# The fifth product of an expert's first layer over 128 rows of the weight tail in place of 64

## The reference

```
# layer 0: 16 experts, hidden width 384, top 4 by softmax
h = einsum('nh,ech->nec', t, mlp1_w) + mlp1_b        # 192 -> 768 (gate and linear part)
a = min(glu, 7) * sigmoid(1.702 * glu) * (clip(lin, -7, 7) + 1)
out = sum_e comb[n, e] * (a_e @ mlp2_w_e.T + mlp2_b_e)   # 384 -> 192
# layer 1: 8 experts, hidden width 768, top 1
out = sum_e comb[n, e] * (relu(x @ wi_e) @ wo_e)         # 192 -> 768 -> 192
```

## Time and profile before

| | |
|---|---|
| median of 3 runs | 606.01 us (605.06 to 611.18) |
| the profiled execution: span, first to last instruction | 613.5 us (the page gives no other time of it) |
| matmuls busy | 536.5 us, 87% of the span |
| weight loads busy | 444.9 us, 73% |
| DVE busy | 349.5 us, 57% |
| ACT, POOL busy | 213.7 us, 170.6 us |
| up(0) of layer 0 starts, layer 0's last add ends | 123.9 us, 368.9 us |
| up(0) of layer 1 starts, last down ends | 446.9 us, 610.7 us |

### The profile page before, as it was taken

The page is one execution under the profiler, slowest core; times in us unless marked ns, Lnnn a source line. Parts: engine busy times, 40 slices in busy tenths (PEclk is TensorE's granted clock), DMA queues, the critical chain, the costliest instruction groups (busy, mean ns, idle before and its releaser), DMA issues.

```text
span 613.5 us, 9611 instructions
## 1 busy us (share of the span) xinstructions
PE 536.5 (87%) x3471; PEld 444.9 (73%) x3471; DVE 349.5 (57%) x678; ACT 213.7 (35%) x344; POOL 170.6 (28%) x104
## 2 busy tenths in 40 slices
PE   5799969699899999999999997602597999999998
PEld 5446956487788888888888883202385998899988
DVE  1340156558687877877777663997527733333332
ACT  0011131245355455455455431702223234223230
POOL 1100021205244444444444114240004442144110
PEclk9755558689799999999999986555558999999999
DMA  8200001002222222222222310010001202221001
GB/s 334 91 0 0 1 1 52 1 1 72 72 72 71 71 71 71 71 71 71 73 88 88 124 41 0 0 51 1 1 0 65 92 25 91 91 90 38 1 1 28
DMA packets 8843, 33.41 MB, mean 54 GB/s; under 512 B 961, under 2 KB 1762, under 8 KB 8818
## 3 DMA queue, kind: packets, MB, share of 16 engines
q1 hardware_dynamic: 8674, 33.00, 15.7%
q10 hardware_dynamic: 144, 0.07, 0.1%
HBM read 32.65 MB, written 0.42 MB: 54 GB/s over the span
## 4 chain that ended last, share of the span: by engine, by line
PE 63%; DVE 11%; issue 1%; ACT 1%; DVEq 0%
PE ps L1194 35%; PE ps L1056 26%; DVE hs L977 1%; DVE prod L972 1%; DVE rmat L957 1%; DVE aval L842 1%; DVE h L806 1%; DVE stats L580 1%; PE ps L1041 0%; PE ps L1045 0%; DVE rmat L961 0%; DVE above L658 0%; DVE bsq L948 0%; DVE qx L944 0%; PE ps L1248 0%
## 5 line engine op out<-in xcount | busy, mean ns | idle before, releaser
L525 POOL TENSOR_TENSOR w_lo<-raw,w_hi 128x768 fp32r<-128x768 f32 x48 | 100.1, 2108 | 310.1 <-ACT w_hi L329 310.1
L1056 PE MATMUL ps<-w_hi,hid_hi 128*119 128x192 f32 (+1 forms) x480 | 129.3, 269 | 0.0
L1056 PE MATMUL ps<-w_lo,hid_hi 128*119 128x192 f32 (+1 forms) x480 | 127.4, 265 | 0.0
L1056 PE MATMUL ps<-w_hi,hid_lo 128*119 128x192 f32 (+1 forms) x480 | 127.3, 265 | 0.0
L1056 PEld LDWEIGHTS ps<-w_hi,hid_hi 128*119 128x119 f32 (+1 forms) x480 | 84.7, 176 | 3.5 <-issue 0.4
L806 DVE SCALAR_TENSOR_TENSOR h<-ps,comb,h 119x192 f32<-119x192 f32 (+1 forms) x120 | 49.8, 415 | 65.1 <-PE ps L1056 61.7
L1056 PEld LDWEIGHTS ps<-w_lo,hid_hi 128*119 128x119 f32 (+1 forms) x480 | 84.7, 176 | 0.0
L1056 PEld LDWEIGHTS ps<-w_hi,hid_lo 128*119 128x119 f32 (+1 forms) x480 | 84.6, 176 | 0.0
L1194 PE MATMUL ps<-xa_hi,w_hi 128*128 128x272 f32 x288 | 76.6, 349 | 7.2 <-DVE hid_lo L1012 3.9
L1194 PE MATMUL ps<-xb_hl,w_lo 64*128 64x272 f32 x288 | 76.6, 347 | 0.0
L1012 DVE SCALAR_TENSOR_TENSOR hid_lo<-ps,hid_hi 128x544 fp32r<-128x544 f32 x48 | 34.6, 725 | 55.2 <-ACT hid_hi L499 55.1
(11 more groups left out here) (183 smaller groups left out, 704.0 us busy)
## 6 DMA issues: line engine op xcount, KB each, us to landing
raw<-in_w SPq DMA_DIRECT2D x24, 768.0 KB, 5.5
raw<-in_w SPq DMA_DIRECT2D x16, 288.0 KB, 2.8
raw<-in_w SPq DMA_DIRECT2D x8, 576.0 KB, 3.8
xp_sb<-in_xp SPq DMA_DIRECT2D x4, 357.0 KB, 5.6
pk_sb<-in_pk SPq DMA_DIRECT2D x1, 970.0 KB, 8.2
pk_sb<-in_pk SPq DMA_DIRECT2D x1, 851.5 KB, 9.0
tokw_sb<-in_tokw SPq DMA_DIRECT2D x1, 672.0 KB, 4.5
out_rows<-h SPq DMA_DIRECT2D x4, 89.2 KB
```

Of the source, the lines that this page charges most:

```text
L525: pool.tensor_tensor(w1_lo[k][:, a:a + W1C], raw1[k][:, a:a + W1C], w1_hi[k][:, a:a + W1C].bitcast(F32), ALU.subtract).then_inc(s["w1_lo"], 1)
L1056: ins = pe.matmul(dst, a, b, start=(n == 0), stop=(n == len(pairs) - 1), skip_group_check=True)
```

## The change

The last entry of `parts` takes all 128 rows of both operands: `w1_lo[:, b]` against `xb_hl[:]`. Rows 64 to 127 add lo(weight)·lo(token) of the tail to the sum, a product that was left out before. The count, the order, the columns and the waits of all matmuls stay as they are; 24 experts x 6 groups x 2 halves = 288 matmuls and their weight loads change in rows.

```
                     parts = [(hi[:, a], xa_hi[:]), (hi[:, b], xb_hl[:]), (hi[:, a], xa_lo[:]), (lo[:, a], xa_hi[:]),
-                             (lo[0:KB, b], xb_hl[0:KB, :])]
+                             (lo[:, b], xb_hl[:])]
```

## The result

| | before | changed |
|---|---|---|
| median, runs of the first comparison | 605.67 us (4 runs, 605.06 to 611.18) | 569.51 us (4 runs, 567.20 to 570.13) |
| ratio | | 0.934 (0.929 to 0.940) |
| again, beside the experiments | 615.04 us (7 runs, 608.12 to 621.14) | 569.00 us (4 runs, 566.63 to 575.22) |
| ratio | | 0.927 (0.920 to 0.935) |
| profiled execution, span | 613.5 us | 565.4 us (its time 567.20) |

The change makes the kernel 6.6 to 7.3% faster. The kernel before scatters widely: its 52 runs in this study lie between 599.2 and 621.3 us with a median of 610.8, the 8 runs of the changed kernel between 566.6 and 575.2 with a median of 569.1. So the saving is 36 us in one comparison and 46 in the other, and where the difference comes from has to be read in the traces.

The account below looks back on a forecast made before the run. PE's pace was taken to bound both expert layers. Savings of 28.8 us in layer 0 and 17.5 in layer 1, together 46.3, came off the 606.0 median: 559.7, say 560, range 551 to 575.

Parts of the forecast that it names:

- the price of the fifth product: In each group of up, changing between 128 and 64 rows costs 0.40 us; at full height the product takes 0.25.
- PE's own periods: Steady periods with PE alone: 12.08 us in layer 0 (from 14.42) and 16.6 in layer 1 (from 18.94).
- Rival 1: The gap comes from the fifth product's place or the overlapping-load rule, not rows; nothing won, 606 us; 2%.
- The wait of 0.40 us through POOL and low(2): Layer 0, steady: PE waits 0.40 us at group 3 for gate(0), behind POOL's w1 split and DVE's low(2); period 12.48.
- no wait and no DMA changes: Whole kernel: the edit only takes 288 matmuls and their loads from 64 rows to 128, altering no wait or DMA.
- 12 x 1.94 = 23.3: Layer 0, up(3) to up(14): twelve periods each 1.94 us shorter, 23.3 us saved.
- Layer 1: Up(2) to up(7) save 6 x 2.34 = 14.0 us, with no wait on another engine near; layer sum 17.5.
- 2.2 + 1.0: Layer 0's opening: 2.2 us from up(0) and up(1), 1.0 from three later groups, partly at the lower clock.
- 2.5 + 1.0: Layer 1's opening: up(0) ends 2.5 us earlier at the lower clock; the three groups after the wait save 1.0.
- 2 (DVE-bound, 572): Layer 0 turns DVE-bound, wait 1.4 us in place of 0.4, 12 us less won, 572 us; 15%.
- 3 (no wait): Layer 0's path through POOL is shorter, so no wait, and the openings gain a little more; 553 us; 8%.
- 4 (the clock falls by PE's waits in the steady part): Layer 0: PE's waits lower the granted clock; all twelve periods at half clock give 686 us, slower than before; 1%.

Follow-up runs that it names:

- b_pairs: Kernel before, with the 64-row product put first in odd groups so that two stand side by side; 587.91 us, ratio 0.968.
- a_loads: Changed kernel, with SP issuing each w1 load an expert earlier, ahead of its wait for the w2 split; 562.64 us, ratio 0.916.
- a_again: The changed kernel run once more, unaltered, beside the experiments; 569.00 us, ratio 0.927.
- b_loads: Kernel before, with only SP's order altered so that w1 loads are issued an expert earlier; 612.48 us beside 610.67 for the kernel before.
- a_both: Changed kernel, with w1 loads issued an expert earlier and DVE doing gate(0) before low(2); 557.06 us, ratio 0.907.
- a_halves: a_loads with each of POOL's two operations on w1 cut into two of 384 columns; 552.27 us, ratio 0.899.
- a_four: Changed kernel without the fifth product, so four products a group; 559.42 us, ratio 0.919.
- a_96: Changed kernel, with the fifth product over 96 rows in place of 128; 561.09 us in its one run.
- a_gate: Changed kernel, with DVE doing gate(0) before low(2) of the previous expert; 567.39 us, ratio 0.927.
- b_both: Kernel before, with w1 loads issued an expert earlier and gate(0) before low(2); 609.53 us, ratio 1.010.

## Why the prediction was right or wrong

**What bounds the kernel, and the price of the fifth product: right.** 0.40 a group for two changes of height was read from the earlier trace rows and is confirmed by three kernels: all full height 1.25, pairs of 64-row products half the saving, 96 rows none of the cost. PE's own periods were forecast as 12.08 and 16.60; they are 12.07 and 16.63. Rival 1 (nothing won) is excluded by b_pairs.

**The wait of 0.40 us through POOL and low(2): right, but not the longest.** a_loads shows it by itself, 0.35 a period, and so do the two periods of 12.42 and 12.41 in the changed kernel, in which the loads came in time. The step that failed is the sentence that nothing else moves, "no wait and no DMA changes", and with it "12 x 1.94 = 23.3": the loads of w1 were not costed. It could have been read off before: SP issued load1 at 262.89 and ACT started that expert's split at 269.17, 6.3 us later (6.0 in the periods beside it), with 5.5 us as the median time to landing on the page. By an estimate, a period 1.94 shorter leaves 4.1 to 4.3. What was missing is 0.57 us a period in the mean, 12 x 0.57 = 6.8 us; a_loads against a_again measures 6.4.

**Layer 1: right.** 2.31 a period for 2.34, no other wait, as argued from ACT's 0.62 and DVE's 0.72.

**The openings: the size wrong, by the clock.** The terms 2.2 + 1.0 and 2.5 + 1.0 took the stretches at the lower clock as of equal length. In the two profiled executions they weren't, and the openings gave 8 us more; the stretches at the lower clock were 6.8 us shorter in layer 0's opening and some 11 in layer 1's, of which half counts, about 9 us. This was luck of these two executions, and it hides the 6 us missing in layer 0 when spans are compared; what the openings gain on equal clocks isn't settled to better than a few microseconds. With b_loads' 20.4 us in place of 25.3, layer 1's first stretch gives 1.8 where 2.5 was forecast.

**Total.** Right would have been 46.3 - 6.8 = 39.5: 606 - 39.5 = 566.5, or from the median of all 52 runs 571.3; measured were 569.5 and 569.0. Both lie between the two; the median of the first three runs, 606.0, is 4.8 us below that of all 52. In the first comparison, where the kernel before had 605.7, 3 us stay unexplained, which is within what the openings scatter. The forecast itself, 560, was 9.5 us low. That 569.5 lies in the range of 551 to 575 is owed to the width taken for a DVE-bound layer and a longer wait through POOL, not to any thought of the loads.

**Rivals.** 2 (DVE-bound, 572) came nearest in the number and was wrong in the mechanism: DVE is no bound at 12.07. 3 (no wait) didn't come by itself, but a_both and a_halves are that kernel: 557 and 552 for 553 forecast. 4 (the clock falls by PE's waits in the steady part) did not come: the page's clock line has 9 throughout layer 0's steady part, with waits of up to 1.2 us there. But falls of this kind do occur there: four in `a_four` at waits of 2.3 to 4.3 us, one in `a_96` after a wait of 1.87 (and none in `a_gate`, with waits of up to 2.58).

## What to carry to other kernels

A product over half the rows among products of full height is dearer than one of full height: useful data in the other rows cost nothing (zeros there were not run), and where the rows can't be filled, put the 64-row products side by side. When a change shortens a period, write down the issue-to-use distance of every load in it, not only the waits that the profile shows: a transfer with 6.3 us of room for 5.5 is the next wait. Where a VectorE operation with two inputs in SBUF meets GpSimd's on the path of the kernel, try GpSimd's in pieces: here VectorE waited for the end of the running one, and the pieces cost GpSimd 5.07 us for 4.28.

## What the runs showed of the hardware that I had not expected

A product over 96 rows behaves as one of full height (0.25 us from start to start), one over 64 has 0.10 more ahead of it, 0.19 more up to the next product and 0.11 more behind that one, and by b_pairs this is the price of the two changes of height, 0.20 each, and not of the 64 rows. DVE's clamp, with one input in SBUF, can be held as well: 1.49 us in a_halves (at 249.48, beside POOL's split of w2) in place of 0.43. The load of 768 KB issued at 274.66 was in use without a wait 4.5 us later, others (261.70, 248.12) took 5.7 and 6.0 in the same kernel; what makes them differ stays open. Where the granted clock rises in layer 1's opening differs by 10 us and more between executions: 15 us into up(0) in the trace before, 8 in b_pairs, 3 to 5 in the other twelve, b_both and b_loads with the old fifth product among them. The start of up(0) in layer 0 moves too: 113.5 us in a_96 and 124.0 in the changed kernel, from which a_96 differs in its fifth product alone. No run of this study tells why.
